# Attention over 16-wide heads: scores as two float32r products over 32 rows instead of one float32 product

## The reference, cut to what matters

```python
def _L1_xattn_ref(x, context, w_qkv, w_proj, b_proj):
    H, D = 16, 16
    qkv = (x @ w_qkv.T).reshape(B, N, 3, H, D).transpose(2, 0, 3, 1, 4)
    q, k, v = (qkv[0], qkv[1], qkv[2])
    kv = context.reshape(B, N_c, 2, H, D).transpose(2, 0, 3, 1, 4)
    k = jnp.concatenate([kv[0], k], axis=2)
    v = jnp.concatenate([kv[1], v], axis=2)
    attn = jnp.einsum('bhnd,bhmd->bhnm', q * D ** -0.5, k)
    attn = jax.nn.softmax(attn, axis=-1)
    out = jnp.einsum('bhnm,bhmd->bhnd', attn, v)
    return out.transpose(0, 2, 1, 3).reshape(B, N, C) @ w_proj.T + b_proj
```

## Time and profile before

| | |
|---|---|
| Median of 3 runs | 2725.27 us (2724.52 to 2727.11) |
| The profiled execution | 2728.62 us |
| Its span in the trace | 2726.7 us |
| The changed stage in the trace | scores from 466.0 to about 806 us |
| Mean granted TensorE clock | 0.955 |

### The profile page before, as it was taken

How to read it: one execution, slowest core, us unless ns; L and a number is a source line. 1 busy time by engine, 2 the same in 40 slices (tenths; PEclk the granted TensorE clock), 3 DMA queues, 4 the chain that set the end, 5 groups by cost and what they waited for, 6 DMA issues and landing times. The chain is left out here.

```text
span 2726.7 us, 38491 instructions
## 1 busy us (share of the span) xinstructions
PE 2361.6 (87%) x15045; PEld 1680.3 (62%) x15045; DVE 1294.5 (47%) x2609; ACT 995.9 (37%) x2834; POOL 128.2 (5%) x206
## 2 busy tenths in 40 slices
PE   6778887999988999989999999969988897874984
PEld 4455555666655666666666666547876675654773
DVE  6456665777764334333455445654443443231003
ACT  3245564777762111112333333433223442231122
POOL 0000000000000000000000000030010000002003
PEclk8979999999998999999999999999999999796996
DMA  3000001000002000020000000000011000021332
GB/s 113 16 1 1 1 1 40 13 25 13 24 1 93 1 0 1 1 109 8 9 9 9 8 9 1 1 28 0 1 43 40 20 5 16 1 72 61 124 113 66
DMA packets 52534, 74.81 MB, mean 27 GB/s; under 512 B 8050, under 2 KB 41348, under 8 KB 51204
## 3 DMA queue, kind: packets, MB, share of 16 engines
q1 hardware_dynamic: 50820, 68.14, 7.4%
q0 software_dynamic: 1536, 4.20, 0.5%
HBM read 63.94 MB, written 8.39 MB: 27 GB/s over the span
## 5 line engine op out<-in xcount | busy, mean ns | idle before, releaser
L862 ACT ACTIVATE ca_prob<-bank,ca_nmax 128x512 f32<-128x512 f32 x256 | 174.0, 690 | 92.9 <-DVE ca_nmax L929 92.9
L929 DVE TENSOR_REDUCE ca_nmax<-bank 128x1 f32<-128x512 f32 x256 | 164.0, 682 | 56.2 <-PE bank L720 56.1
L862 ACT ACTIVATE na_prob<-bank,na_nmax 128x257 f32<-128x257 f32 x256 | 118.0, 474 | 191.0 <-DVE na_nmax L929 191.0
L1458 PE MATMUL bank<-XN,rf_W 128*128 128x512 f32 x384 | 172.9, 601 | 0.0
L1469 PE MATMUL bank<-rf_W,rf_h 128*128 128x256 f32 x768 | 170.8, 379 | 0.0
L1469 PEld LDWEIGHTS bank<-rf_W,rf_h 128*128 128x128 f32 x768 | 145.9, 190 | 33.1 <-issue 14.8
L734 PEld LDWEIGHTS bank<-cst,ca_prob 128*128 128x128 f32 x1024 | 112.3, 142 | 73.6 <-issue 63.2
L862 ACT ACTIVATE ra_prob<-bank,ra_nmax 128x256 f32<-128x256 f32 x256 | 118.2, 482 | 104.1 <-DVE ra_nmax L929 104.1
L1513 ACT ACTIVATE rf_r<-bank 128x512 f32<-128x512 f32 x96 | 57.4, 598 | 256.3 <-PE bank L1458 256.3
L734 PE MATMUL bank<-cst,ca_prob 128*128 128x128 f32 x1024 | 140.5, 279 | 6.6 <-DVE ca_pT L935 5.9
L929 DVE TENSOR_REDUCE na_nmax<-bank 128x1 f32<-128x257 f32 x256 | 90.8, 417 | 91.5 <-PE bank L720 91.5
(11 more groups left out here) (395 smaller groups left out, 4423.8 us busy)
## 6 DMA issues: line engine op xcount, KB each, us to landing
xl_w<-in_L_ffn_w SPq DMA_DIRECT2D x16, 1024.0 KB
dp_cx<-in_ctx_tok SPq DMA_DIRECT2D x4, 1024.0 KB, 14.1
ca_v<-in_ctx_values SPq DMA_DIRECT2D x8, 512.0 KB, 4.6
rf_W<-in_L_ffn_w SPq DMA_DIRECT2D x8, 512.0 KB, 8.6
na_Wkv<-in_L_xattn_Wkv SPq DMA_DIRECT2D x1, 4096.0 KB
na_cxT<-in_ctx SPq DMA_DIRECT2D x8, 512.0 KB, 3.4
ma_cxT<-in_ctx SPq DMA_DIRECT2D x8, 512.0 KB, 3.3
X<-in_x SPq DMA_DIRECT2D x1, 2048.0 KB, 7.9
```

Of the source, the lines that this page charges most:

```text
L862: e = act.activation(prob[:, n % 2, u, hh * keys:(hh + 1) * keys], S[u][:, hh * keys:(hh + 1) * keys], ACT.Exp, bias=nmax[:, n % 2, u, hh: ...
L929: v.tensor_reduce(nmax[:, n % 2, u], S[u][:, 0:W].rearrange("p (h k) -> p h k", h=per), AX.X, ALU.max, negate=True).then_inc(maxed, 1)
L1458: mm = pe.matmul(g.bank[n % 3][:], W1[:, k, c * P:(c + 1) * P], g.XN[:, k, gi * GT:(gi + 1) * GT], start=(k == 0), stop=(k == KD - 1))
```

## The change

Keys and queries are each split into a rounding (float32r) and a rest. In `ca_k_halves`, for the even heads, the 16 rows of the head hold the keys' roundings and the other head's 16 rows hold the same keys' rests (for the odd heads the reverse), so 32 rows give key rounding and key rest at once. The queries' halves hold the head's own roundings (part 0) or rests (part 1) in both groups of 16 rows. A score is then the sum of two float32r products over 32 rows in the same bank. GpSimd makes roundings and rests (a copy that rounds, and a subtraction). The rows that belong to the other 16 partitions are moved by DMAs from SBUF to SBUF, which SP issues: 16 for the queries of a batch (32 KB each) and 8 for its keys (64 KB each). The queries are scaled once and kept as `ca_q`. The first batch's load moves into `prefetch`, and the first half of the first key split into `prepare`. The diff, blank lines left out:

```diff
--- before.py
+++ after.py
@@ -552,7 +552,8 @@
 def attention_stream(g, ctx, tag, heads, dh, groups, keys, front, front_at, q_of, k_of, v_of, slot_of, project, finish,
-                     wl, n_weights, mask=None, own_keys=False, load=None, n_loads=0, load_after=None, null=None, reg=None):
+                     wl, n_weights, mask=None, own_keys=False, load=None, n_loads=0, load_after=None, null=None, reg=None,
+                     stack=None):
@@ -588,11 +589,14 @@
         g.sem(f"{tag}_{n}") for n in ("scored", "maxed", "exped", "turned", "copied_by_vector", "copied_by_scalar",
                                       "shared_ready", "freed_by_vector", "freed_by_scalar", "valued", "inverted",
                                       "widened", "scaled"))
-    ld = [g.sem(f"{tag}_loaded{j}") for j in range(2)] if n_loads else None
+    ld = [g.sem(f"{tag}_loaded{j}") for j in range(2)] if n_loads and stack is None else None
+    if stack is not None:
+        ld = stack.loaded
     S = [g.bank[u] for u in range(4)]
     TB = [g.bank[4], g.bank[5]]
     M, O = g.bank[6], g.bank[7]
     INV = 2 if reg is not None else 1
+    q_parts = 1 if stack is None else 2
     SC = 2 if reg is not None else 1
     if null is not None:
@@ -674,15 +678,40 @@
             if n_loads:
                 for b in range(B):
                     if b >= 2:
+                        if stack is not None:
+                            stack.move_queries(sp, b)
                         load_after(sp, b - 2, ready, ready_at, valued, R)
-                    for d in load(sp, b):
-                        d.then_inc(ld[b % 2], 16)
+                    if stack is None or b >= 1:
+                        for d in load(sp, b):
+                            d.then_inc(ld[b % 2], 16)
+                    if stack is not None and b >= 1:
+                        for early in range(0 if b == 1 else b, b + 1):
+                            if early < 2:
+                                stack.move_queries(sp, early)
+                            stack.move_keys(sp, early)
             sp.wait_ge(wl, 16 * n_weights)
         @block.gpsimd
         def _(po):
+            def split_keys_and_queries(b):
+                wait_freed(po, ("front", b, 0))
+                if b >= 2:
+                    po.wait_ge(scored, 4 * R * (b - 1))
+                stack.split_queries(po, b)
+                if b >= 1:
+                    po.wait_ge(ld[b % 2], 16 * n_loads * (b // 2 + 1))
+                    stack.split_keys(po, b, slice(0, N))
+                wait_freed(po, ("front", b, 1))
+                stack.split_keys(po, b, slice(N, 2 * N))
+            if stack is not None:
+                split_keys_and_queries(0)
             for n in range(NR):
                 f, r2 = divmod(n, RF)
+                if stack is not None and n % R == 0 and n // R + 1 < B:
+                    split_keys_and_queries(n // R + 1)
                 if null is not None:
                     b, r = divmod(n, R)
                     if r == 0 and b >= 2:
@@ -706,6 +735,8 @@
                     wait_front(pe, b)
                     if n_loads:
                         pe.wait_ge(ld[b % 2], 16 * n_loads * (b // 2 + 1))
+                    if stack is not None:
+                        stack.wait_stacked(pe, b)
                 for u0 in range(0, 4, GA):
                     for u in range(u0, u0 + GA):
                         i, a, hs = unit(n, u)
@@ -715,12 +746,15 @@
                             ml, mr = mask(i, b, hs)
                             pe.matmul(S[u][:, 0:W], ml, mr, start=True, stop=False, skip_group_check=True)
                     for hh in range(per):
-                        for u in range(u0, u0 + GA):
-                            i, a, hs = unit(n, u)
-                            mm = pe.matmul(S[u][:, hh * keys:(hh + 1) * keys], q_of(hs[hh], i, b), k_of(hs[hh], i, b),
-                                           start=(mask is None), stop=(hh == per - 1), skip_group_check=True)
-                            if hh == per - 1:
-                                mm.then_inc(scored, 1)
+                        for part in range(q_parts):
+                            for u in range(u0, u0 + GA):
+                                i, a, hs = unit(n, u)
+                                q = q_of(hs[hh], i, b) if q_parts == 1 else q_of(hs[hh], i, b, part)
+                                last = hh == per - 1 and part == q_parts - 1
+                                mm = pe.matmul(S[u][:, hh * keys:(hh + 1) * keys], q, k_of(hs[hh], i, b),
+                                               start=(mask is None and part == 0), stop=last, skip_group_check=True)
+                                if last:
+                                    mm.then_inc(scored, 1)
             def turn(n, f):
                 fill = FILLS * n + f
@@ -1321,6 +1355,63 @@
+class HalfStack:
+    def __init__(self, g, sb):
+        self.q = sb("q", [P, KD, N])
+        self.q_halves = sb("q_halves", [P, 2, 2, KD, 2, N], F32R)
+        self.k_halves = sb("k_halves", [P, 2, KD, 2, 2 * N], F32R)
+        self.k_rest = sb("k_rest", [P, KD, 2 * N], F32R)
+        self.loaded = [g.sem(f"ca_loaded{j}") for j in range(2)]
+        self.queries_split, self.keys_split = g.sem("ca_queries_split"), g.sem("ca_keys_split")
+        self.queries_moved = [g.sem(f"ca_queries_moved{j}") for j in range(2)]
+        self.keys_moved = [g.sem(f"ca_keys_moved{j}") for j in range(2)]
+    def split_queries(self, po, b):
+        own = self.q[:].unsqueeze(2).to_broadcast([P, KD, 2, N])
+        rounded, rest = self.q_halves[:, 0, b % 2], self.q_halves[:, 1, b % 2]
+        po.tensor_copy(rounded, own).then_inc(self.queries_split, 1)
+        po.wait_ge(self.queries_split, 2 * b + 1)
+        po.tensor_tensor(rest, own, rounded, ALU.subtract).then_inc(self.queries_split, 1)
+    def split_keys(self, po, b, of):
+        k, rounded = self.keys[:, b % 2, :, of], self.k_halves[:, b % 2, :, :, of]
+        done = 4 * b + (0 if of.start == 0 else 2)
+        po.tensor_copy(rounded, k.unsqueeze(2).to_broadcast([P, KD, 2, N])).then_inc(self.keys_split, 1)
+        po.wait_ge(self.keys_split, done + 1)
+        if b >= 1:
+            po.wait_ge(self.keys_moved[(b - 1) % 2], 16 * 8 * ((b - 1) // 2 + 1))
+        po.tensor_tensor(self.k_rest[:, :, of], k, rounded[:, :, 0], ALU.subtract).then_inc(self.keys_split, 1)
+    def move_queries(self, sp, b):
+        sp.wait_ge(self.queries_split, 2 * b + 2)
+        for part in range(2):
+            of = self.q_halves[:, part, b % 2]
+            for s in range(0, P, 32):
+                for odd in range(2):
+                    at, to = s + 16 * odd, s + 16 * (1 - odd)
+                    sp.dma_start(of[to:to + 16, :, odd].bitcast(F32), of[at:at + 16, :, odd].bitcast(F32))\
+                      .then_inc(self.queries_moved[b % 2], 16)
+    def move_keys(self, sp, b):
+        sp.wait_ge(self.keys_split, 4 * b + 4)
+        for s in range(0, P, 32):
+            for odd in range(2):
+                at, to = s + 16 * odd, s + 16 * (1 - odd)
+                sp.dma_start(self.k_halves[to:to + 16, b % 2, :, odd].bitcast(F32), self.k_rest[at:at + 16].bitcast(F32))\
+                  .then_inc(self.keys_moved[b % 2], 16)
+    def wait_stacked(self, pe, b):
+        pe.wait_ge(self.queries_moved[b % 2], 16 * 16 * (b // 2 + 1))
+        pe.wait_ge(self.keys_moved[b % 2], 16 * 8 * (b // 2 + 1))
 def context_attention_layer(g):
     nc, A = g.nc, g.A
     with ExitStack() as ctx:
@@ -1328,45 +1419,65 @@
         Wqkv = sb("Wqkv", [P, KD, 3 * D])
         Wp = sb("Wp", [P, KD, D])
         bias = sb("bias", [P, KD])
-        qz = sb("qz", [P, 2, 2, KD, N])
         kk = sb("k", [P, 2, KD, 2 * N])
         vv = sb("v", [P, 2, 4, 2 * D])
         wl, zeroed = g.sem("ca_weights"), g.sem("ca_zeroed")
+        stack = HalfStack(g, sb)
         def prefetch(sp):
             sp.dma_start(Wqkv[:], feature_rows(A["L1_xattn_w_qkv"])).then_inc(wl, 16)
             sp.dma_start(Wp[:], feature_rows(A["L1_xattn_w_proj"])).then_inc(wl, 16)
             sp.dma_start(bias[:], A["L1_xattn_b_proj_col"]).then_inc(wl, 16)
+            for d in load(sp, 0):
+                d.then_inc(stack.loaded[0], 16)
         def prepare(po):
             for j in range(2):
                 po.memset(vv[:, j, 2:4], 0.0).then_inc(zeroed, 1)
             po.wait_ge(zeroed, 2)
-        layer_norm_phase(g, "n1x", prefetch=prefetch, prepare=prepare)
+            po.wait_ge(stack.loaded[0], 32)
+            stack.split_keys(po, 0, slice(0, N))
         def load(sp, b):
             yield sp.dma_start(kk[:, b % 2, :, 0:N], feature_rows(A["ctx"][0:D, b * N:(b + 1) * N]))
             yield sp.dma_start(vv[:, b % 2, 0:2],
                                A["ctx_values"][b * N:(b + 1) * N, :].rearrange("(t p) d -> p t d", p=P))
+        stack.keys = kk
+        layer_norm_phase(g, "n1x", prefetch=prefetch, prepare=prepare)
```

(22 more changed lines are left out.)

## The result

| | us |
|---|---|
| Before, median of 5 runs (with the 3 above) | 2726.31 (2724.52 to 2728.26) |
| Changed kernel, median of 5 runs | 2716.94 (2706.27 to 2717.48) |
| Ratio changed to before | 0.9958, 95% interval 0.9941 to 0.9974 |
| The same two kernels again, other runs (e5 below) | 2720.01 and 2725.63, ratio 0.9978, interval 0.9965 to 0.9992 |
| Forecast | 2718.4, against a median before of 2725.3 |

The account below looks back on a forecast made before the run. The prediction took a serial ring of scores, maximum and exponentials as the bound, not busy TensorE. -22.8 (rounds) + 14.4 (start) + 1.5 (clock) = -6.9 us gave 2718.4 us against 2725.3; 8-in-10 range 2709 to 2742 us.

Parts of the forecast that it names:

- The ring: Plain round of scores, maximum, exponentials: shortens by the score block's whole saving, 0.40 us, from 5.27 to 4.87 us.
- Side by side in float32r: Score block: float32r products run side by side in four row groups, 0.71 to 0.76 us instead of 1.14.
- rivals A and B: Score block: float32r no faster than float32, 2741 us, chance 0.08; or groups take turns, about 2803 us, chance 0.04.
- Rival D: Score block: a wave steps by 278 ns, block 0.84 us, total 2724 us; chance 0.14.
- 57 of 64 rounds: Changed stage: round 2 gains nothing in seven batches, so 57 rounds x 0.40 = 22.8 us saved.
- the clock's loss: First rounds after the start's wait: TensorE at half clock costs 1.5 us, bounds 0 and 2.4.
- VectorE, ScalarE, GpSimd at 0: Changed stage: the dropped tensor_scalar, new waits and GpSimd's splits change the time by 0 us.
- Moves hidden in the middle: Between batches: splits, issues and landings finish before the next batch's scores, with slack of 5.6 us.
- Issues over 0.7 us apart: SP's move issues: a spacing this wide was named as a sign of the prediction being wrong.
- the turning point: Move chain in the middle: moves decide the time from an issue spacing of 0.73 us.
- The start: Before the first batch's scores: uncovered splits and 24 moves delay them by 14.4 us, bounds 12 and 18.
- The sum: Whole program: -22.8 + 14.4 + 1.5 = -6.9 us.

Follow-up runs that it names:

- e5: The changed kernel once more, unedited, against the kernel before; 2720.01 us, ratio 0.9978.
- e3: Changed kernel with one float32 product on the same halves instead of two float32r products, queries' rests left out; 2742.22 us, ratio to before 1.0056.
- e7: Changed kernel with every move cut into two of 8 partitions, 48 issues per batch instead of 24, same bytes; one run, 2850.47 us.
- e4: Changed kernel with 36 float32 products keeping TensorE busy in the wait before the first scores; 2722.18 us, ratio to before 0.9978.
- e2: Changed kernel with the first batch's scores in float32 from masked queries, as before the change; 2707.30 us, ratio to before 0.9927.
- e6: Changed kernel with the first batch's 8 key moves issued from ScalarE's queue beside SP's query moves; 2716.92 us, ratio to before 0.9969.
- e8: Changed kernel with VectorE scaling outT behind the following round's first two maxima instead of ahead; 2724.63 us, ratio to before 0.9994.
- e1: Changed kernel without all 192 moves, so the keys' rests do not reach the products; 2700.42 us, ratio to before 0.9908.

## Why the prediction was right

Its direction, its mechanism and its time held: 2718.4 forecast, 2716.9 and 2720.0 measured. Point by point, the forecast's step first:

- **The ring.** Right. Block 0.71 to 0.76 us: 0.74. Plain round 4.87: 4.87. The idle time that ScalarE leaves to TensorE is unchanged (0.23 and 0.51 us).
- **Side by side in float32r.** Right, and rivals A and B fall at the same row: 47.9 us for 64 blocks. The block sits between the two prices that were taken from rows, 2 x 0.213 and 2 x 0.235 plus 0.29. Rival D, with the Trainium skill's 3.07 times ("TensorE: Matmul & The Clock Gate", packing small matmuls), would need 0.84 us a block; this trace has 0.74, so float32r agrees with the bfloat16 rows and not with that figure.
- **57 of 64 rounds.** Right. Round 2 kept its 5.55 us, and a batch is 40.3 us for 40.2. First and last scores came 21.3 us closer, the clock's loss included.
- **VectorE, ScalarE, GpSimd at 0.** Right: e3's batches grew by 0.03 us with all splits and moves in place.
- **Moves hidden in the middle.** Right, with less cover than stated: 2.9 to 4.4 us in the seven batches and not 5.6. Issues over 0.7 us apart, which the prediction had named as a sign of being wrong, came in the query moves of three batches (0.71 to 0.74) and did no harm. Counted from one batch's first scores (562.43): queries split at +9.4 us (forecast 10.2), last query move issued at +19.9 (18.4, the issues being 0.65 us apart and not 0.51), load landed at +24.7 (23.5), keys split at +29.5 (28.4), last key move issued at +34.6 (32.5) and landed at +36.3 (34.6), against the next batch at +40.3 (40.2). e7 shows what lies past the turning point.
- **The start.** The term mis-sized: 17.3 us for 14.4. The 0.51 us per issue came from loads of 256 and 512 KB from HBM; 24 moves within SBUF took 0.64 each, 3.1 us more. The landing was 2.3 us for 2.6. The clock's loss in batch 0 was 1.9 us for 1.5 (e4), of which 1.3 came 15 us after the first scores, where I had not looked, and where the kernel before loses as much.
- **The sum.** The forecast had -6.9 us for the program: -22.8 + 14.4 + 1.5. From the first front product to the last scores the traces have 17.3 - 21.3 = -4.0 us, with the last block -4.4. That is 2.5 us less gain than forecast: the start took 2.9 more and the rounds gave 0.5 less, and the clock cost 0.9 less (0.6 net for 1.5). The 21.3 hold both kernels' clock: 1.9 us lost after the wait (e4), 1.3 lost in round 3 of before (6.56 us for 5.27); without either it would be 21.3 + 1.9 - 1.3 = 21.9, for the 56 x 0.40 = 22.4 of the forecast that lie between first and last scores; the last block's 0.4 is the 57th. Behind the scores another 1.6 us are clock in the normalization, and 6.0 us of the spans' difference lie in layers that the change does not touch; the forecast had no term for either. The medians' agreement within 1.6 us is therefore partly luck; that of the stage, -4.4 for -6.9, is the fair measure of the working.

## What to carry to other kernels

A busy engine is not the bound as long as it idles once a round: find the ring (scores, maximum, exponential) and price a change by its share of it, then look for the one round in which another wait hides the gain. Small DMAs cost by the number of issues on one queue; put them where a batch of other work covers them, and give the first batch, which nothing covers, the old code (e2: 364.3 us for the layer instead of 379.3). Compare layers of two traces cut at fixed products before reading a difference of a few microseconds in the total.

## What the runs showed of the hardware

- float32r products of 32 rows and 512 columns run side by side in the four row groups: eight in 0.74 us.
- Back-to-back issues from SP came 0.51 us apart for loads from HBM, 0.64 for moves of 16 partitions within SBUF (0.71 to 0.74 on the average in some batches), 0.73 for moves of 8. SP and ScalarE issued side by side at 0.65 us each (e6). Moves of 32 KB landed 2.0 us after issue, of 64 KB 2.3.
- GpSimd wrote 1024 float32r values per partition in 1.04 us from float32 and subtracted 1024 in 2.37 us; VectorE's reductions from PSUM kept their mean of 682 ns.
- After an idle time of 18 us TensorE ran at 1.2 GHz (granted clock 0.50) for 5.0 us more, and once more for 3.4 us some 15 us after the first scores. The kernel before, e2, e5 and e8 have a like dip in round 3 (6.56 us instead of 5.27 in the kernel before, which had no long wait); e1, e3, e4 and e6 have none. Why is open.
